# A two-layer graph network kernel: the third-order correction of a reciprocal root written as a product chain on VectorE, with rank copies, POOL's extras and the last tile's staging rows moved

## What is computed

```python
# layer 0, per graph: x [512,128], adj [512,512], about 6% of it nonzero
adj = adj + eye; dis = adj.sum(axis=2) ** -0.5
h = layernorm(x + dis * (adj @ (dis * (x @ w0))) + b0)
# layer 1
m_j, m_i = h @ W1[:D], h @ W1[D:]
pre[i, j] = m_j[j] + m_i[i] + b1                      # 512 x 512 x 128
msg[i, j] = gelu(layernorm(pre[i, j]) * g1 + be1)     # exact gelu
agg[i] = sum_j adj[i, j] * msg[i, j]
out = layernorm(h + layernorm([h, agg] @ W2 + b2) * g2 + be2)
```

## Time and profile before

| what | value |
|---|---|
| median of 3 runs | 3537.92 us (3535.61 to 3540.91) |
| the profiled execution | 3535.7 us, its span 3533.7 us |
| busy PE, PEld | 3198.2 us (91%), 2943.3 us (83%) |
| busy DVE, ACT, POOL | 3008.2 us (85%), 3042.6 us (86%), 2104.7 us (60%) |
| mean granted PE clock | 0.973 of full speed |
| L939, L942 on DVE | 88.1 us, 92.0 us, 128 times each |
| L663, L666 on ACT | 79.2 us, 92.4 us, 128 times each |

### The profile page before, as it was taken

The page is one execution under the profiler, slowest core; times in us unless marked ns, Lnnn a source line. Parts: engine busy times, 40 slices in busy tenths (PEclk is TensorE's granted clock), DMA queues, the critical chain, the costliest instruction groups (busy, mean ns, idle before and its releaser), DMA issues.

```text
span 3533.7 us, 87356 instructions
## 1 busy us (share of the span) xinstructions
PE 3198.2 (91%) x26504; PEld 2943.3 (83%) x26505; DVE 3008.2 (85%) x6816; ACT 3042.6 (86%) x8038; POOL 2104.7 (60%) x2628
## 2 busy tenths in 40 slices
PE   4899999999989998999998999989999999999988
PEld 2788888888878888888887888888888888888887
DVE  3689988889978898888898888988888988888987
ACT  3788889898968988888987989888889898989887
POOL 3556665556645566655566555666555666555652
PEclk7999999999989999999999999999999999999999
DMA  2333333233332333323332323333323333323231
GB/s 73 106 98 106 104 115 106 88 107 106 101 102 83 110 106 97 123 94 96 111 107 94 109 87 106 107 97 122 102 89 111 106 98 121 108 82 111 91 96 45
DMA packets 284214, 355.29 MB, mean 101 GB/s; under 512 B 28208, under 2 KB 242736, under 8 KB 283696
## 3 DMA queue, kind: packets, MB, share of 16 engines
q1 hardware_dynamic: 250928, 231.55, 22.5%
q0 software_dynamic: 32768, 117.47, 8.8%
HBM read 223.09 MB, written 125.83 MB: 99 GB/s over the span
## 4 chain that ended last, share of the span: by engine, by line
PE 50%; DVE 22%; issue 10%; ACT 10%; POOL 6%; DMA 1%; DVEq 1%; ACTq 0%; SPq 0%; POOLq 0%; PEldq 0%
PE agg_even_ps L1323 9%; PE z_even_ps L1364 8%; PE z_odd_ps L1364 8%; PE agg_odd_ps L1323 6%; DVE pick L1078 6%; DVE spread L1107 4%; POOL table L514 3%; DVE msg L1053 2%; PE z_even_ps L1360 2%; PE z_odd_ps L1360 2%; ACT tmp L713 2%; ACT root L658 2%; PE p_ps L1175 2%; PE p_ps L1244 2%; PE agg_odd_ps L1244 2%
## 5 line engine op out<-in xcount | busy, mean ns | idle before, releaser
L713 ACT ACTIVATE tmp<-nbr,r_sb 128x128 f32<-128x128 f32 x4032 | 1262.5, 389 | 24.9
L1078 DVE SCALAR_TENSOR_TENSOR pick<-rank,root_p 128x512 f32<-128x512 bf16 (+3 forms) x1536 | 914.8, 625 | 98.3 <-PE z_odd_ps L1364 53.2
L514 POOL DMA_INDIRECT table<-stage,row_id x512 | 747.0, 1459 | 155.8 <-issue 145.1
L1107 DVE SCALAR_TENSOR_TENSOR spread<-nbr 128x512 f32<-128x512 bf16 (+3 forms) x1536 | 814.8, 557 | 6.5 <-PE agg_even_ps L1323 5.5
L698 ACT ACTIVATE msg<-msg 128x768 f32<-128x768 f32 x768 | 646.7, 842 | 16.0 <-issue 8.3
L529 POOL COPY root_extra<-root_p 128x32 f32<-128x32 f32 (+4 forms) x768 | 315.7, 411 | 518.7 <-ACT root_p L672 514.7
L1364 PEld LDWEIGHTS z_odd_ps<-mi_g,pick 128*128 128x128 f32 x4608 | 587.1, 198 | 26.0 <-issue 0.5
L1323 PE MATMUL agg_odd_ps<-spread,msg 128*128 128x128 f32 x4608 | 597.5, 281 | 4.5 <-issue 3.6
L1364 PE MATMUL z_odd_ps<-mi_g,pick 128*128 128x129 f32 x4608 | 600.6, 282 | 0.0
L1364 PEld LDWEIGHTS z_even_ps<-mi_g,pick 128*128 128x128 f32 x4608 | 567.1, 192 | 25.6 <-issue 0.2
L1364 PE MATMUL z_even_ps<-mi_g,pick 128*128 128x129 f32 x4608 | 579.0, 275 | 0.0
(11 more groups left out here) (219 smaller groups left out, 4609.4 us busy)
## 6 DMA issues: line engine op xcount, KB each, us to landing
nbr<-table SPq DMA_DIRECT2D x128, 640.0 KB, 5.0
adj_g<-in_adj SPq DMA_DIRECT2D x32, 1024.0 KB, 5.9
nbr_root<-table SPq DMA_DIRECT2D x128, 256.0 KB, 5.4
nbr_extra<-table SPq DMA_DIRECT2D x384, 70.0 KB
nbr_extra<-table SPq DMA_DIRECT2D x128, 90.0 KB
nbr_extra<-table SPq DMA_DIRECT2D x256, 40.0 KB
x_g<-in_x SPq DMA_DIRECT2D x32, 256.0 KB, 3.1
table<-stage,row_id POOLq DMA_INDIRECT x512, 4.6
```

The costliest lines, as they stand in the source:

```text
L514: pool.indirect_dma_start(table[q], bass.IndirectOffsetOnAxis(ap=row_id[:, jt * TB + it:jt * TB + it + 1], axis=0), stage[:, jt, it, :], N ...
L713: last = act.activation(tmp[:, c % 2, n - FROM[u], :], half_row, ACT.Identity, scale=r_sb[:, c % 2, n - FROM[u]:n - FROM[u] + 1])
L1078: ins = dve.scalar_tensor_tensor(into.rearrange("p k n -> p (k n)"), rank[:, it % 2, span], float(MARK + t), root_p[:, it % 2, span], ALU. ...
L1107: ins = dve.scalar_tensor_tensor(into, ranks(nbr[:, it, jt:jt + count, A_RANK:A_ROOT]), float(MARK + t), nbr[:, it, jt:jt + count, A_ADJ:A ...
```

## The change

The step was: h = seed^2, u = (var + eps) * h (DVE), a square with bias and scale (ACT), and (that + rest) * seed (DVE). It becomes three DVE products, in place in the staging rows. The seed is taken with a scale, so that the cubic's factor is 1: with t = (var + eps) * s^2 the result is ((t + c1) * t + c2) * s. ACT's second square goes away; its first square now writes into the staging rows, and waits for the scatters that read them. `half` is gone; tile 3's rows have a second home, used by every other graph.

```diff
-CUBE_K = math.sqrt(0.375)
-CUBE_REST = 1.875 - 0.375 * (5 / 3) ** 2
+SEED_K = 0.375 ** 0.2
-T_RANK, T_ROOT, T_EXTRA = 3, 4, (6, 6, 5, 6)
+T_RANK, T_ROOT, T_EXTRA = 3, 4, (6, 6, 5, 8)
...
-        half = sb("half", [P, TB, N])
...
-        stage = sb("stage", [P, TB, TB, ROW])
+        rows_sb = sb("rows_sb", [P, TB, TB, ROW])
+        last_rows = sb("last_rows", [P, TB, ROW])
...
+        def stage(q, jt):
+            return last_rows[:, :, :] if jt == TB - 1 and q else rows_sb[:, jt, :, :]
+        def halfway(q, jt):
+            return stage(q, jt)[:, :, A_ROOT:ROW]
+        def written(jt, a):
+            return max(a - 1, 0) if jt == TB - 1 and isinstance(a, int) else a - 1 if jt == TB - 1 else a
...
@@ POOL, s == S_SUP + 1 @@
-                    own = half[:, 0, :].rearrange("p (t o) -> p t o", t=TB)
+                    own = sqi[:, :].rearrange("p (t o) -> p t o", t=TB)
...
@@ POOL, steps @@
-                if a is not None:
-                    prepare(a, (i + AHEAD) // GC % 2 ^ 1, s)
                 k, t = cx.sorted(i)
                 if k is not None:
                     sort(cx.tiles + k, k, t)
                 if a is not None:
+                    prepare(a, (i + AHEAD) // GC % 2 ^ 1, s)
                     scatter(a, (i + AHEAD) // GC % 2 ^ 1, s)
...
@@ ACT, s == S_AT + jt; POOL's L487 likewise @@
-                                act.wait_ge(p_scat[jt][it], a * 16)
+                                act.wait_ge(p_scat[jt][it], written(jt, a) * 16)
...
@@ ACT, seed and squares @@
-                    act.activation(root[:, :, :], var[:, :, :], ACT.Abs_reciprocal_sqrt, bias=eps_col[:, :]).then_inc(p_seed, 1)
+                    act.activation(root[:, :, :], var[:, :, :], ACT.Abs_reciprocal_sqrt, bias=eps_col[:, :], scale=SEED_K ** -2).then_inc(p_seed, 1)
...
-                        act.activation(half[:, jt, :], root[:, jt, :], ACT.Square).then_inc(p_sq, 1)
-                    if s == S_ROOT + jt:
-                        act.wait_ge(p_new, a * TB + (jt + 1))
-                        act.activation(half[:, jt, :], half[:, jt, :], ACT.Square, bias=cube_col[:, :], scale=CUBE_K).then_inc(p_cube, 1)
+                        if not is_int(a, 2 if jt == TB - 1 else 1):
+                            for it in range(TB):
+                                act.wait_ge(p_scat[jt][it], written(jt, a) * 16)
+                        act.activation(halfway(q, jt), blocks(root[:, jt, :]), ACT.Square).then_inc(p_sq, 1)
...
@@ ACT, steps @@
+                k, t = cx.sorted(i)
+                if k is not None and s == S_SEED:
+                    sort(cx.tiles + k, k, t)
                 if a is not None:
                     prepare(a, (i + AHEAD) // GC % 2 ^ 1, s)
-                k, t = cx.sorted(i)
-                if k is not None:
+                if k is not None and s != S_SEED:
                     sort(cx.tiles + k, k, t)
...
@@ DVE @@
-                    if (s, slot) == (S_ROOT + jt, 0):
+                    if (s, slot) == (S_ROOT + jt, 2):
                         dve.wait_ge(p_sq, a * TB + (jt + 1))
-                        dve.scalar_tensor_tensor(half[:, jt, :], v, EPS, half[:, jt, :], ALU.add, ALU.mult).then_inc(p_new, 1)
-                    if (s, slot) == (S_ROOT + jt + 1, 0):
+                        dve.scalar_tensor_tensor(halfway(q, jt), blocks(v), EPS, halfway(q, jt), ALU.add, ALU.mult).then_inc(p_new, 1)
+                    if (s, slot) == (S_ROOT + jt, 3):
+                        dve.wait_ge(p_new, a * TB + (jt + 1))
+                        dve.scalar_tensor_tensor(halfway(q, jt), halfway(q, jt), -10 / 3 * SEED_K ** 2, halfway(q, jt),
+                                                 ALU.add, ALU.mult).then_inc(p_cube, 1)
+                    if (s, slot) == (S_ROOT + jt, 4):
                         dve.wait_ge(p_cube, a * TB + (jt + 1))
-                        dve.scalar_tensor_tensor(stage[:, jt, :, A_ROOT:ROW], half[:, jt, :].rearrange("p (i n) -> p i n", i=TB), CUBE_REST,
-                                                 y.rearrange("p (i n) -> p i n", i=TB), ALU.add, ALU.mult).then_inc(p_mask, 1)
+                        dve.scalar_tensor_tensor(halfway(q, jt), halfway(q, jt), 5 * SEED_K ** 4, blocks(y), ALU.add, ALU.mult).then_inc(p_mask, 1)
```

More of the change, by code:

```diff
@@ L116, in adj_resnorm_kernel @@
         eps_col = sb("eps_col", [P, 1])
-        cube_col = sb("cube_col", [P, 1])
         ones_b = sb("ones_b", [P, P], BF16)
@@ L263, in adj_resnorm_kernel, with blocks @@
         N_CONST = 3 + 7 + 1
-        N_IDENT = 15 + sum(len(slot) for _, slot in PIECES)
+        N_IDENT = 14 + sum(len(slot) for _, slot in PIECES)
         XL = len(LOADS) * 16
+        def stage(q, jt):
+            return last_rows[:, :, :] if jt == TB - 1 and q else rows_sb[:, jt, :, :]
+        def halfway(q, jt):
+            return stage(q, jt)[:, :, A_ROOT:ROW]
+        def blocks(row):
+            return row.rearrange("p (i n) -> p i n", i=TB)
+        def written(jt, a):
+            return max(a - 1, 0) if jt == TB - 1 and isinstance(a, int) else a - 1 if jt == TB - 1 else a
         def ranks(rows):
@@ L425, in _ @@
             pool.memset(halves[:, D - 1:D], 0.5).then_inc(s_ident, 1)
-            pool.memset(eps_col[:, :], EPS).then_inc(s_ident, 1)
+            pool.memset(eps_col[:, :], EPS / SEED_K ** 2).then_inc(s_ident, 1)
             pool.memset(minus_half[:, :], -0.5).then_inc(s_ident, 1)
-            pool.memset(cube_col[:, :], -CUBE_K * 5 / 3).then_inc(s_ident, 1)
-            pool.wait_ge(s_ident, 8)
+            pool.wait_ge(s_ident, 7)
             pool.affine_select(out=ident[:, :], in_=ident[:, :], compare_op=ALU.not_equal, fill=1.0,
@@ L467, in prepare @@
                     if not is_int(a, 1):
-                        wait_alone(pool, p_mask, a * TB)
+                        wait_alone(pool, p_fill, a * NF - (NF - F_MIT - 1))
                     pool.tensor_tensor(own, sup[:, :, :], dis[:, :].unsqueeze(2).to_broadcast([P, TB, D]), ALU.mult).then_inc(p_own, 1)
@@ L483, in prepare @@
                     for jt in range(TB):
-                        if not is_int(a, 1):
+                        if not is_int(a, 2 if jt == TB - 1 else 1):
                             for it in range(TB):
-                                wait_alone(pool, p_scat[jt][it], a * 16)
-                        last = pool.tensor_copy(stage[:, jt, :, A_MJ:A_RANK], mj_g[:, jt, :].unsqueeze(1).to_broadcast([P, TB, D]))
+                                wait_alone(pool, p_scat[jt][it], written(jt, a) * 16)
+                        last = pool.tensor_copy(stage(q, jt)[:, :, A_MJ:A_RANK], mj_g[:, jt, :].unsqueeze(1).to_broadcast([P, TB, D]))
                     last.then_inc(p_copy, 1)
@@ L514, in scatter @@
                     pool.indirect_dma_start(table[q], bass.IndirectOffsetOnAxis(ap=row_id[:, jt * TB + it:jt * TB + it + 1], axis=0),
-                                            stage[:, jt, it, :], None).then_inc(p_scat[jt][it], 16)
+                                            stage(q, jt)[:, it, :], None).then_inc(p_scat[jt][it], 16)
             def sort(n, k, t):
@@ L597, in prepare @@
                         filled(F_AT + jt)
-                        if not is_int(a, 1):
+                        if not is_int(a, 2 if jt == TB - 1 else 1):
                             for it in range(TB):
-                                act.wait_ge(p_scat[jt][it], a * 16)
-                        act.copy(stage[:, jt, :, A_ADJ:A_MJ], p.rearrange("p (i n) -> p i n", i=TB)).then_inc(p_ev, 1)
+                                act.wait_ge(p_scat[jt][it], written(jt, a) * 16)
+                        act.copy(stage(q, jt)[:, :, A_ADJ:A_MJ], p.rearrange("p (i n) -> p i n", i=TB)).then_inc(p_ev, 1)
                 for jt in range(TB):
@@ L604, in prepare @@
                         act.wait_ge(r_fill, a * TB + (jt + 1))
-                        act.copy(ranks(stage[:, jt, :, A_RANK:A_ROOT]), t_ps[:, 0, :].rearrange("p (i n) -> p i n", i=TB)).then_inc(r_ev, 1)
+                        act.copy(ranks(stage(q, jt)[:, :, A_RANK:A_ROOT]), t_ps[:, 0, :].rearrange("p (i n) -> p i n", i=TB)).then_inc(r_ev, 1)
                 if s == S_SUP:
@@ L1174, in prepare @@
                         for mt in range(TB):
-                            last = mm(dst, stage[:, mt, it, A_ADJ:A_MJ], sup[:, mt, :], start=(mt == 0), stop=(mt == TB - 1))
+                            last = mm(dst, stage(q, mt)[:, it, A_ADJ:A_MJ], sup[:, mt, :], start=(mt == 0), stop=(mt == TB - 1))
                     if s == S_PROD + 1:
```

## The result

The changed kernel takes **3567.83 us** (median of 4 runs, 3566.61 to 3572.89) where the kernel before, beside it, takes 3539.41 (4 runs, 3535.61 to 3546.71). The ratio is 1.0081, with an interval of 1.0061 to 1.0100: slower by 28 us. The forecast was 3602 us, slower by 66. The loss came where it was forecast and at its forecast size; a gain at another place was three times as large as I had it.

A forecast was written before the change was run, and what follows sets the result against it. PE bounds the ordinary stretch, DVE some 18 us a graph around the seed. The profiled 3535.7 us, plus 86.8 (31 x 2.80) for DVE's longer path, minus 20 for waits for scatters, gave 3602 us; range 3520 to 3640.

The forecast's parts named there:

- Steps 1 to 4: Seed's stretch, path to z of unit 14: 0.70 - 1.00 + 1.24 + 1.86 = 2.80 us a graph, +86.8 us.
- Step 2: DVE at i = 10: three picks move into the wait for the square (-1.00 us), two further products join the path (+1.24).
- Step 3: DVE behind the seed: POOL's additions block spread and second product as they blocked the picks; 2.2 us a graph kept.
- Step 4: DVE, steps 11 to 13: one product more each, +1.86 us a graph; the product gone from step 14 saves nothing.
- Step 5: ACT's second square gone, 92.4 us of busy time: counted 0, since DVE has no idle time in these steps.
- Step 6: Tile 3's second home and x_v's power ahead of the extras: 20 us off, bounds 0 and 67; extras' move costs 0.
- Rival A: Seed's stretch: POOL's additions end before DVE's products, 2.2 us a graph leave the path; with 67 us off, 3488; chance 0.17.
- B: Nothing changes: POOL's additions no longer block DVE's products, but only 20 us come from the second home; 3535 us; chance 0.08.
- Rival C: Seed's stretch: PE's slow clock reaches units where PE is the bound, roughly 1 us a graph, 3634 us; chance 0.13.
- D: DVE's first product waits for the square as long as before, near 3.9 us; already in the sum, no chance given.
- over 2 us a graph: Sign that the forecast is wrong: the time saved between units 19 and 24 exceeds 2 us a graph.

## Why the forecast was right and wrong

- **Steps 1 to 4 (+2.80 us a graph, +86.8):** the sum was right, at +2.83 measured. That it was right to 0.03 us is luck: its terms were some 0.3 us off in opposite directions. The rank copy ahead was put at 0.70; before against the old step in the new kernel shows 33.21 - 32.77 = 0.44, and that includes that kernel's other edits. The products less the picks were put at 1.24 + 1.86 - 1.00 = 2.10; undoing them gave 2.39.
- **Step 2:** the picks fell into the wait, at 0.62 and 0.55 us, and the wait stayed 3.87 us where "near 3.9" was forecast.
- **Step 3 (the port, 2.2 us kept):** shown. Taking POOL's additions away from the products gave 2.02 us. The spread and the second product stood where the picks had stood.
- **Step 4:** one product more in each of steps 11 to 13, and nothing saved in step 14: unit 14 is 3.90 us long in the median graph of both kernels.
- **Step 5 (ACT's square, 0):** ACT's busy time fell by 72 us, and the path grew by what the products cost. The path was DVE's; counting its instructions alone gave 2.10 us where undoing the products and bringing the square back gave 2.39.
- **Step 6 failed, and it alone.** "I take 20 us off" was 57 us, and the cause named was the wrong one. The second home, to which I gave the 20, is worth nothing in this kernel: with one home and the extras in their new place ACT waits 15.7 us for scatters instead of 7.3, and the time is the same (1.0089 beside 1.0081). Of the 44.4 us of rows 8, 28 went in the kernel with neither edit, and it lost more than that again at `dis`. The extras' move, which I put at "Cost 0" because "those start no later, as the order only swaps neighbours", is the whole gain: without it 57 us are lost. Nor was the reason given right: the addition to pre_g and the edges do start later, 7.98 us into unit 19 in after and 5.03 with the extras back, and that is what helps. Two things were overlooked. I did not ask on which of DVE's instructions POOL's long ones would come to lie, though step 3 of the same text had just priced that at 2.2 us. And the wait of sup for `dis` (37.0 us, 23 times) was in the list of waits of before and did not enter the sum, so that the upper bound of 67 was built from another wait.
- **Rival A** (ports open, 3488) did not happen, nor B: L507 ended at 1140.02, behind the start of the second product at 1138.81. **Rival C** (the clock): the stretch of units 8 to 14 grew by 2.83 us where the instructions alone give 2.80; over 16 us from just ahead of the table load, the granted clock is 0.89 in after as it was in before. Its price of roughly 1 us was too low: a unit's 12 z matmuls are busy for 1.5 us (598.2 + 589.2 us over 768 units). **D**: the wait for the square stayed, at 3.87 us.
- What was to prove the forecast wrong, "over 2 us a graph" saved between units 19 and 24, came within 0.2 us of being met: 1.84 us were saved there.

## What to carry to other kernels

When two engines exclude each other on a port, the order of one engine's stream sets the speed of the other's. So when instructions are moved, lay the moved engine's long ones over the other's stream as it will then stand, and look at what waits behind the instructions they will cover; swapping neighbours is not free of effect. Before work is moved from one engine to another in a stretch, find who owns that stretch: here three products on DVE cost 71 us against two and a square on ACT, because DVE owned it. And when a wait is to be removed, look in the list of waits for the next one on the same engine: here 28 us of one wait went and 35 us of the next came, and only when both went did the kernel gain.

## What the hardware showed that was not expected

**A stall once in most graphs, on two of the five chips that the experiments ran on.** Both kernels take about 100 us more there. It sits mostly in units 17 and 18 (6.89 us elsewhere, 12.0 in the kernel before there). With POOL's `res` one step earlier in before it sits in unit 14 in 8 graphs, so it is not bound to one place in the program. No semaphore is named for its gaps. In the graph shown the core moves 232 GB/s over 0.69 of its DMA engines' time, against 188 over 0.49 in the same unit elsewhere; over the stalled unit 14 of another graph it is 158 over 0.41. On one of these chips four kernels came out equal that take 3497 to 3625 us elsewhere. An experiment on waits should not be judged by its ratio alone when the kernel beside it is at another level than before; the unit table showed where to look.

**The price of a port is paid in whole instructions.** The second product took 1.76 us beside POOL's addition and 0.68 alone, and two picks of 512 took 3.17 us beside POOL's addition and edges and 1.43 beside the power and small copies. The Trainium skill (SBUF — State Buffer, Who interferes with whom) states this exclusion for a DVE instruction with two SBUF inputs and a GpSimd one that reads SBUF; both pairs of numbers agree with it, for f32 products as well as for picks.
